# First attention's queries: three single passes over split operands instead of one fp32 product

## What is computed

```python
qp = einsum('bld,ed->ble', layernorm(x), Wq)
idx = argmax(einsum('bld,bmd->blm', qp, kv), axis=-1)
mem = take_along_axis(kv, idx[..., None], axis=1)
mk, mv = split(einsum('bld,ed->ble', mem, Wkv), 2, axis=-1)
attn = softmax(einsum('bhld,bmd->bhlm', heads(qp), mk) * scale)
x = x + einsum('bld,ed->ble', attn @ mv, Wc)
```

## Time and profile before

| | us |
|---|---|
| median of 3 runs | 1908.39 (1903.99 to 1915.61) |
| profiled execution, its own time | 1909.73 |
| its span, first to last instruction | 1907.9 |
| TensorE busy in the span | 1720.9 |
| VectorE busy | 1284.1 |
| ScalarE busy | 1136.5 |
| mean granted TensorE clock, as a share of full | 0.947 |

### The profile page before, as it was taken

The page is one execution under the profiler, slowest core; times in us unless marked ns, Lnnn a source line. Parts: engine busy times, 40 slices in busy tenths (PEclk is TensorE's granted clock), DMA queues, the critical chain, the costliest instruction groups (busy, mean ns, idle before and its releaser), DMA issues.

```text
span 1907.9 us, 41070 instructions
## 1 busy us (share of the span) xinstructions
PE 1720.9 (90%) x15760; PEld 1451.1 (76%) x15760; DVE 1284.1 (67%) x2756; ACT 1136.5 (60%) x2882; POOL 822.8 (43%) x1306
## 2 busy tenths in 40 slices
PE   5789898887999999999999879999999999987648
PEld 3566666666989999999999768788888888866523
DVE  3677887643532888888888386777777777677321
ACT  1356565532336777777777477777777777744210
POOL 3233432111011333333331387888888887654000
PEclk8789999998999999999999999999999999999766
DMA  6754465234786666666676722222222321112699
GB/s 180 202 124 104 107 123 116 61 116 166 263 281 215 246 246 246 243 232 234 244 245 239 234 73 86 71 62 68 90 68 62 92 65 57 43 48 91 233 366 328
DMA packets 140163, 303.81 MB, mean 159 GB/s; under 512 B 14080, under 2 KB 82944, under 8 KB 124736
## 3 DMA queue, kind: packets, MB, share of 16 engines
q1 hardware_dynamic: 116032, 188.68, 32.3%
q0 software_dynamic: 19584, 108.31, 16.8%
q10 hardware_dynamic: 4352, 4.20, 0.6%
HBM read 210.44 MB, written 90.44 MB: 158 GB/s over the span
## 4 chain that ended last, share of the span: by engine, by line
PE 71%; DVE 12%; DMA 5%; issue 5%; POOL 4%; ACT 2%; SPq 1%; POOLq 0%; DVEq 0%; ACTq 0%
PE ps L1230 11%; PE ps L1216 11%; PE ps L1812 5%; PE ps L359 5%; PE ps L223 4%; PE ps L1843 4%; PE ps L1798 4%; PE ps L1832 4%; PE ps L365 3%; DVE NM L578 2%; PE ps L426 2%; DMA rp_scratch<-RP 2%; PE ps L497 2%; PE ps L526 2%; POOL P L213 2%
## 5 line engine op out<-in xcount | busy, mean ns | idle before, releaser
L200 ACT ACTIVATE P<-ps,NM 128x256 f32<-128x256 f32 x512 | 236.2, 481 | 127.5 <-DVE NM L189 127.5
L213 POOL TENSOR_TENSOR P<-P,RS 128x1024 f32<-128x1024 f32 x128 | 242.9, 1903 | 73.7 <-DVE RS L207 73.3
L1216 PE MATMUL ps<-XRP,W1P 128*128 128x256 f32 x1872 | 226.8, 281 | 3.3 <-DVE W1P L1299 3.3
L1216 PEld LDWEIGHTS ps<-XRP,W1P 128*128 128x128 f32 x1872 | 220.1, 190 | 3.6 <-DVE W1P L1299 3.6
L1230 PE MATMUL ps<-W2P,HP 128*128 128x256 f32 x1872 | 221.5, 277 | 0.0
L673 ACT ACTIVATE PT<-ps 128x512 f32<-128x512 f32 x256 | 140.7, 611 | 132.5 <-PE ps L438 132.5
L1230 PEld LDWEIGHTS ps<-W2P,HP 128*128 128x128 f32 x1872 | 218.0, 188 | 0.0
L578 DVE TENSOR_REDUCE NM<-ps 128x2 f32<-128x512 f32 x256 | 164.3, 684 | 64.1 <-PE ps L426 63.9
L189 DVE TENSOR_REDUCE NM<-ps 128x2 f32<-128x512 f32 x256 | 164.6, 684 | 5.6 <-PE ps L1798 4.1
L1150 POOL DMA_INDIRECT WE<-in_we,WIX x39 | 44.2, 1135 | 278.5 <-DVE W1P L1299 209.2
L1259 ACT ACTIVATE HF<-ps,WE 128x256 f32<-128x256 f32 x312 | 129.0, 465 | 43.3 <-PE ps L1216 43.3
(11 more groups left out here) (219 smaller groups left out, 3710.2 us busy)
## 6 DMA issues: line engine op xcount, KB each, us to landing
KS<-k_scratch SPq DMA_DIRECT2D x64, 256.0 KB, 3.1
V<-v_scratch SPq DMA_DIRECT2D x16, 1024.0 KB, 6.3
rp_scratch<-RP SPq DMA_DIRECT2D x16, 1024.0 KB, 8.8
R<-rp_scratch SPq DMA_DIRECT2D x16, 1024.0 KB, 13.9
k_scratch<-KVM SPq DMA_DIRECT2D x52, 256.0 KB, 4.2
QS<-q_scratch SPq DMA_DIRECT2D x96, 128.0 KB, 4.8
v_scratch<-KVM SPq DMA_DIRECT2D x40, 256.0 KB, 3.0
ys_scratch<-YS SPq DMA_DIRECT2D x39, 256.0 KB, 8.2
```

The lines of the kernel that those rows point to most:

```text
L200: i = e.activation(self.P[u % 4][:, c, :], PS[SB[n % 3]][:, y * 256:y * 256 + 256], ACT.Exp, bias=self.NM[:, u % 4, c:c + 1], accum_out=se ...
L213: e.tensor_tensor(p, p, self.RS[:, u % 4, :].unsqueeze(2).to_broadcast([128, 4, 256]), ALU.mult).then_inc(self.s_pn, 1)
L1216: m = e.matmul(PS[p][:, hh * 256:hh * 256 + 256], W1P[i % 2][wi][:, cc * 1024 + hc * 128:cc * 1024 + hc * 128 + 128], XRP[i % 2][xi][:, cc ...
```

## The change

The turned rows and the weights are each kept as two f32r tiles, a high half that ScalarE's copy makes and a low half, original minus high half, by VectorE. `queries` makes high times high, weight-high times x-low, and weight-low times x-high: twelve single-pass products where four fp32 ones stood. `x_out` now writes the high half and no longer raises `s_mb`; a new VectorE step, `x_low`, reads MB and the high half, writes the low half and raises `s_mb`, which `queries` waits for. It stands in slot 2 behind the maxima and the result's addition. The weights are split once, ahead of the first batch: ScalarE's copy is its first instruction, VectorE's subtraction comes right after the second batch's `norms`. The semaphores of the copies and of the memsets are shared with the new steps.

```diff
-    XNT = mem("XNTa", [128, 2, 256], fp32)
+    XNT = [mem(f"XNTa{i}", [128, 2, 256], f32r) for i in range(2)]
+    WQP = [mem(f"WQP{i}", [128, 2, 256], f32r) for i in range(2)]
...
         def queries(b):
             w.wait_ge(d_w0_w1, 16)
             w.wait_ge(s_mb, use_b["q", b])
+            w.wait_ge(s_mw, 4)
             for ec in range(2):
                 for cc in range(2):
-                    i = e.matmul(MB[:, ec * 256:ec * 256 + 256], WQ[:, cc, ec * 128:ec * 128 + 128], XNT[:, cc, :],
-                                 start=(cc == 0), stop=(cc == 1))
+                    for x, (wi, xi) in enumerate(PAIRS):
+                        i = e.matmul(MB[:, ec * 256:ec * 256 + 256], WQP[wi][:, cc, ec * 128:ec * 128 + 128], XNT[xi][:, cc, :],
+                                     start=(cc == 0 and x == 0), stop=(cc == 1 and x == 2))
             i.then_inc(s_qm, 1)
...
+        def x_low(b):
+            w.wait_ge(s_xqh, 2 * b + 1)
+            e.tensor_tensor(flat(XNT[1][:, :, :]), MB[:, :], flat(XNT[0][:, :, :]).bitcast(fp32), ALU.subtract).then_inc(s_mb, 1)
+
         def queries_low(b):
-            w.wait_ge(s_qh0, b + 1)
+            w.wait_ge(s_xqh, 2 * b + 2)
...
         norms(1)
+        w.wait_ge(s_mw, 3)
+        e.tensor_tensor(flat(WQP[1][:, :, :]), flat(WQ[:, :, :]), flat(WQP[0][:, :, :]).bitcast(fp32), ALU.subtract).then_inc(s_mw, 1)
+        x_low(0)
         queries_low(0)
         best(0)
+        x_low(1)
         queries_low(1)
...
+            elif r == 2 and is_batch(g + 2):
+                x_low(g + 2)
             elif r == 4 and is_batch(g + 2):
                 queries_low(g + 2)
...
         def x_out(b):
             w.wait_ge(s_xt, b + 1)
             w.wait_ge(s_qm, b)
-            e.activation(flat(XNT[:, :, :]), MB[:, :], ACT.Copy).then_inc(s_mb, 1)
+            e.activation(flat(XNT[0][:, :, :]), MB[:, :], ACT.Copy).then_inc(s_xqh, 1)
...
-            e.activation(flat(QH[:, :, :]), MB[:, :], ACT.Copy, scale=0.25).then_inc(s_qh0, 1)
+            e.activation(flat(QH[:, :, :]), MB[:, :], ACT.Copy, scale=0.25).then_inc(s_xqh, 1)
...
+        w.wait_ge(d_w0_w1, 16)
+        w.wait_ge(s_mw, 2)
+        e.activation(flat(WQP[0][:, :, :]), flat(WQ[:, :, :]), ACT.Copy).then_inc(s_mw, 1)
         context_out(0)
...
-        e.memset(CKV[:, :, :], 0.0).then_inc(s_ms, 1)
-        w.wait_ge(s_ms, 1)
-        e.memset(CKV[:, :, 144:145], 1.0).then_inc(s_ms, 1)
+        e.memset(CKV[:, :, :], 0.0).then_inc(s_mw, 1)
+        w.wait_ge(s_mw, 1)
+        e.memset(CKV[:, :, 144:145], 1.0).then_inc(s_mw, 1)
```

More of the change, by code:

```diff
@@ L271, in build @@
     d_ck, d_gk = sem("d_ck"), [sem(f"d_gk{i}") for i in range(2)]
-    s_xn, s_xt, s_qm, s_qh0 = sem("xn0"), sem("xnt0"), sem("qmm0"), sem("q_hi")
+    s_xn, s_xt, s_qm, s_xqh = sem("xn0"), sem("xnt0"), sem("qmm0"), sem("xnt_q_hi")
     s_cm, s_am, s_ix, s_gm = (sem(n) for n in ("ckvmm", "argmm", "argix", "memT"))
-    s_mh, s_wo, s_spl, s_ms = sem("keys0"), sem("outmm0"), sem("ctxsplit"), sem("memsets")
+    s_mh, s_wo, s_spl, s_mw = sem("keys0"), sem("outmm0"), sem("ctxsplit"), sem("memsets_wq")
     s_sc0, s_mx0, s_nt, s_nx = sem("score0"), sem("rowmax0"), sem("maxT"), sem("maxT_out")
@@ L689, in context_out @@
             w.wait_ge(s_gm, b if b > 1 else 0)
-            w.wait_ge(s_ms, 2)
+            w.wait_ge(s_mw, 2)
             w.wait_ge(d_ck, 16 * b)
```

## The result

The changed kernel takes 1920.1 us (median of 8 runs, 1913.8 to 1928.0), the one before 1906.6 beside it: the ratio is 1.0072, with a 95% interval of 1.0043 to 1.0101. The forecast was 1916, from 1905 to 1925. The change costs 8 to 19 us.

What follows compares the result with a forecast made beforehand. Bound: TensorE and VectorE paths meeting at slot 4's maxima. Terms 4.05 - 0.3 + 1.0 = +4.8, clock +2.6, total +7.4 on 1909.73 gives 1917.1; that execution lay 1.3 above the median, so 1916 us, range 1905 to 1925.

Steps and rivals of the forecast that it cites:

- What bounds: Slots 2 to 4: nearly equal TensorE and VectorE paths meet at slot 4's maxima; the change shortens TensorE's, lengthens VectorE's.
- The products: In queries, twelve f32r products take 1.60 us instead of 1.82 at full clock, saving 0.22 us a batch.
- x_low: In slot 2, the added subtraction shifts VectorE's work behind it by 0.67 us.
- L129's stretch: In the statistics, groups 5 to 9: POOL's L770 stretches L129; starting later, it gives back 0.28 of 0.67 us.
- Groups 4 to 13: The shift at slot 4's maxima carries whole into the next group: 4.05 us in sum.
- Rival A: At slot 4, TensorE's path decides and x_low hides; every batch gains its saving, 1904 us. Chance 0.14.
- Rival C: In queries, products wait for weight loads and save nothing; the first batches go without 3.2 us: 1919. Chance 0.06.
- Groups 0 to 3: Groups without results and statistics, where VectorE has room: -0.3 us in sum.
- The clock: TensorE's clock in matches: one slow first burst and one more group in which it falls, +2.6 us.
- rival B: In the matches, idle TensorE time makes three or more further groups fall to half clock, up to 1924 us. Chance 0.2.
- The start: Before slot 0: first queries start 1.6 us later, their burst shortens to 2.90 us; +1.0 us, batch 1 adds 0.
- The sum: Whole kernel: +4.8 us without the clock's part, +7.4 us with it.

Runs made afterwards that it cites:

- e1: The changed kernel with x_low left out for batches 2 to 15, its products kept: 1915.5 us, ratio 1.0047 to the kernel before.
- e2: The kernel before with its fp32 products, plus x_low in the same place writing a tile nobody reads: 1916.1 us, ratio 1.0045.
- f2: The changed kernel with five unread fp32 products in TensorE's idle time of slot 7, groups 2 to 15: 1917.6 us, ratio 1.0038.
- f3: The kernel before with five unread fp32 products in TensorE's idle time of slot 7: 1903.0 us, ratio 0.9961.
- e3: The changed kernel with batches 0 and 1 made by the fp32 products of before, without x_low: 1923.3 us, ratio 1.0097.
- f4: The changed kernel with the statistics of finished batches moved from slot 3 to slot 7: 1917.0 us, ratio 1.0031.
- g2: The changed kernel with both the unread products in slot 7 and the statistics moved to slot 7: 1906.0 us, ratio 1.0012.
- g4: Only batches 0 and 1 as in the changed kernel, batches 2 to 15 by fp32 products without x_low: 1909.8 us, ratio 1.0019.
- g3: The kernel before with both the unread products in slot 7 and the statistics moved to slot 7: 1905.4 us, ratio 0.9985.
- f1: The changed kernel itself, run again without any edit: 1921.6 us, ratio 1.0067 to the kernel before.
- g1: The kernel before, run again without any edit: 1908.4 us, ratio 1.0012.
- e4: The changed kernel with TensorE's idle time ahead of slot 0 filled by products nobody reads: 1920.2 us, ratio 1.0081.

## Why the prediction was right, and where it was short

**What bounds** held as put: two paths that meet at slot 4's maxima, x_low on VectorE's. e1 and e2 part the two halves of the change and each shows one side: 20.52 without x_low, 20.89 with it whatever the products.

**The products** were sized at 1.60 us and take 1.62. **x_low** was sized at 0.67 and costs 0.66, of which L129's shortening gives 0.28 back in groups 5 to 9, as said; the measured shift is 184.69 - 179.49 against 175.59 - 170.78 from slot 2's maxima, 5.20 against 4.81: +0.39. That L129's stretch was POOL's doing is borne out by the times: it is long (0.45 to 0.48 us in groups 6 to 9) in e1, where it again starts while POOL is still at that instruction (L784 there) and ends with it, at 180.78 and 180.76, and short here.

```profile
179.47 1.29 POOL L784 TENSOR_TENSOR W1K<-WS,W1K 128x512 fp32r<-128x512 f32 x1
...
180.32 0.46 DVE L129 TENSOR_SCALAR LTMP<-MV 128x2 f32<-128x2 f32 x1
```

Groups 4 to 13: 10 x 0.37 = 3.7 us, forecast 4.05.

**Rival A** (TensorE's path decides) is out by e1 and e2. **Rival C** (no saving in the products) is out by 1.62 us.

**Groups 0 to 3** were put at -0.3 us. From the first scores to the turn in group 4 it was 88.8 and 89.5 us before and 89.4 and 89.8 after: +0.5. The recorded working has two slips here that change no result: the saving in group 2 is 0.33 us (86.17 to 88.10 less 1.60), as the 88.50 has it, and the six stretches of L129 are worth 1.7 us, not 1.6.

**The clock** was the term that was too small, and a part of rival B is true. Groups 4 to 13 took 215.5 us before and 221.9 after, by the stretches, +6.4; without the 3.7 of x_low that leaves 2.7 for the clock, where one more group, 1.4, was put in. Three groups fall instead of two, and groups 4 and 8, with other causes, lose 1.4 us more. That these falls hang on the idle time ahead of the matches was forecast in B and is shown by f2 and f3. That a longer period or a shorter query burst makes more of them is not: two fell before, three after, four in e2 with the long burst, two in e3 with the changed kernel's groups.

**The start** was put at 1.0 us, plus one slow burst at 1.2. From the first products to the first scores it is 32.6 us on the mean of the seven executions with the whole changed start (30.9 to 34.1; the changed kernel twice, e1, f2, f4, g2, g4), and 30.2 on the four with the start of before (29.3 to 31.2; the kernel before twice, f3, g3): 2.3. The size was right, the reason given for the slow bursts, the shorter query burst, is not borne out: they come and go with the execution in both kernels, behind bursts of 2.9 and of 3.75 us (f1, g1, e2). Of the 14 matches bursts in the seven 8 are slow, of the 8 in the four 2, too few to tell the starts apart. What decides whether a burst is slow no run here parts.

**The sum.** The mark moved from 373.0 on the mean of two executions to 382.1, +9.0, and it was forecast at +7.4. The medians moved by 13.5. The rest, some 4 us, is in neither part of the executions seen: from the mark on these took 1529.4 and 1532.9 us before and 1525.6 and 1529.7 after, no longer. That part differs between executions by more than is sought: 1524.2 us in g4's, 1538.8 in e1's, the two ends of the fourteen. Their own times (1917.8 and 1918.4) lay below the changed kernel's medians, and that of g1 above its own. Whether the later stages are slower in the usual execution stays open, and so does why e1's median stays 8 us above with an unchanged mark; the interval of the ratio, 8 to 19 us, reaches down to the 9 that are explained. So the median of 1920.1 owes its place in the forecast's range partly to the range's width: it moved by 13.5 us where 7.6 was forecast, from a kernel before that took 1906.6 beside it and not 1908.4.

## What to carry to other kernels

Work taken from the busiest engine is worth what the place where it stood allows: look for the point where two engines' rows meet, and count what the change adds on the other side of it, not the busy shares. An instruction that must be added to a row that ends last can be paid for by moving something else of that row (here the statistics) to a slot where the engine waits. And where a group has a stretch of idle TensorE time ahead of a burst, products that nobody reads can be cheaper than the burst at half clock: that was 4 to 11 us in the kernel before, in one set of runs, the only gain clear of noise over the kernel before; a second set with the statistics moved as well (g3) had the same shorter mark but a ratio that doesn't exclude 1.

## What the runs showed of the hardware

A program's falls of the clock repeated in the executions seen: two of the changed kernel had the same three groups low, two of the kernel before the same two, to 0.1 us, although the turn in group 1 came up to 4 us apart; e4, where it came 4 us earlier than in the first of them, had the changed kernel's three as well. Edits move them to other groups, and not only one that lengthens a group by 0.37 us, as in e2: in g4 and e3 the groups' length is unchanged and others fall (9 instead of 11 and 12; 5 and 9 instead of 5, 6 and 10). A gain at the start of the size of e4's need not show in the time: e4's mark is 1.2 to 3.7 us below the changed kernel's two, and its median isn't lower.
